# A graph network's node update: TensorE turns the new rows one step later, ahead of the second products

## The reference

```
agg = segment_sum(messages, dst)
u   = mish(concat([h, agg]) @ W3 + b3)        # h: 10000 x 512
y   = h + (u @ W4 + b4)
x   = x + layernorm(y) * gamma + beta
h   = relu(layernorm(x))                      # input of the fourth layer, L3
out = x + relu(batchnorm(mean_agg(h) @ W_l.T + b_l + h @ W_r.T))
```

## Time and profile before

| what | value |
|---|---|
| median of 3 runs | 2826.0 us (2825.43 to 2830.35) |
| the profiled execution's own time | 2847.13 us |
| its span | 2845.4 us, granted TensorE clock 0.943 |
| busy: TensorE, VectorE, ScalarE, GpSimd | 2446.0, 1907.5, 1520.3, 1122.4 us |
| node update, steps of pairs 4 to 28 | 13.03 us for a pair |
| node update, steps in the zone | 14.45 us for a pair |

### The profile page before, as it was taken

How to read it: one execution, slowest core, us unless ns; L and a number is a source line. 1 busy time by engine, 2 the same in 40 slices (tenths; PEclk the granted TensorE clock), 3 DMA queues, 4 the chain that set the end, 5 groups by cost and what they waited for, 6 DMA issues and landing times. The chain is left out here.

```text
span 2845.4 us, 45119 instructions
## 1 busy us (share of the span) xinstructions
PE 2446.0 (86%) x13421; PEld 1424.2 (50%) x13421; DVE 1907.5 (67%) x4612; ACT 1520.3 (53%) x2246; POOL 1122.4 (39%) x1908
## 2 busy tenths in 40 slices
PE   1648898799789999898978979989999997998954
PEld 1435564344344455444544537766666664444443
DVE  8838886687568866898863436668888887223343
ACT  7637774354335533454335756668888775232280
POOL 1567744254333322555545511124444444001155
PEclk9669999999999999999988989999999998999976
DMA  5545543488559888666544332233333444001187
GB/s 200 204 139 158 156 143 122 124 202 179 117 131 222 203 150 173 222 220 217 185 157 125 103 95 76 90 105 120 121 118 121 142 142 154 3 6 52 45 289 292
DMA packets 374158, 413.92 MB, mean 145 GB/s; under 512 B 192822, under 2 KB 232037, under 8 KB 371182
## 3 DMA queue, kind: packets, MB, share of 16 engines
q1 hardware_dynamic: 347918, 337.27, 40.2%
q0 software_dynamic: 26080, 74.68, 9.0%
HBM read 172.47 MB, written 198.18 MB: 130 GB/s over the span
## 5 line engine op out<-in xcount | busy, mean ns | idle before, releaser
L215 PE MATMUL s_ps_z<-own_weights,slots 128*128 128x512 f16 x2844 | 638.9, 382 | 7.8 <-PEq L163 7.8
L215 PEld LDWEIGHTS s_ps_z<-own_weights,slots 128*128 128x128 f16 (+1 forms) x2844 | 279.1, 98 | 325.0 <-issue 18.0
L1756 ACT ACTIVATE s_g<-s_g,s_rn 128x512 f32<-128x512 f32 x237 | 169.8, 716 | 226.9 <-POOL s_rn L1615 226.7
L1615 POOL TENSOR_TENSOR s_rn<-s_em,minus_half 128x1 f32<-128x1 f32 x237 | 179.7, 758 | 219.0 <-DVE s_em L1684 211.6
L1665 DVE SCALAR_TENSOR_TENSOR s_g<-s_ps_z,s_f,s_bias 128x512 f32<-128x512 f32 x237 | 177.9, 751 | 103.4 <-PE s_ps_z L215 90.8
L2565 PE MATMUL u_ps_z<-slots,weights 128*128 (+2 forms) x1920 | 215.9, 273 | 4.2 <-PEq L163 4.2
L2701 PE MATMUL z_ps_z<-slots,weights 128*128 128x512 f16 (+1 forms) x960 | 212.3, 381 | 2.4 <-PEq L163 2.4
L2565 PEld LDWEIGHTS u_ps_z<-slots,weights 128*128 128x128 f16 x1920 | 186.4, 98 | 26.9 <-issue 4.4
L2670 DVE BATCH_NORM_STATS2 z_stats<-slots 128x6 f32<-128x512 f32 (+1 forms) x76 | 52.2, 687 | 187.9 <-ACT slots L2687 187.9
L1675 DVE SCALAR_TENSOR_TENSOR s_junk<-s_g 128x512 f32<-128x512 f32 x237 | 164.5, 694 | 4.1
L215 PE MATMUL s_ps_z<-s_wn,s_aT 128*128 128x512 f16 x720 | 165.2, 379 | 1.8 <-DVE s_aT L1498 1.8
(11 more groups left out here) (435 smaller groups left out, 5558.2 us busy)
## 6 DMA issues: line engine op xcount, KB each, us to landing
h_rows<-s_g SPq DMA_DIRECT2D x237, 256.0 KB, 2.7
x_rows<-q_x SPq DMA_DIRECT2D x79, 256.0 KB
s_halves<-x_rows SPq DMA_DIRECT2D x79, 256.0 KB
x_rows<-s_halves SPq DMA_DIRECT2D x79, 256.0 KB
u_x<-x_rows SPq DMA_DIRECT2D x79, 256.0 KB
x_rows<-u_x SPq DMA_DIRECT2D x79, 256.0 KB
h_rows<-u_h SPq DMA_DIRECT2D x79, 256.0 KB
weights<-x_rows SPq DMA_DIRECT2D x79, 256.0 KB
```

The source lines that it names most:

```text
L215: ins = nc.tensor.matmul(out_ap, a(c), w[:, part * size + c * n:part * size + (c + 1) * n], start=first and c == 0 and m == 0, stop=stop a ...
L1615: nc.gpsimd.tensor_tensor(out=self.rn[b][:, :], in0=self.em[b][:, :], in1=minus_half[:, :], op=POW).then_inc(self.s_rn, 1)
L1756: nc.scalar.activation(self.g[b][:, :], self.g[b][:, :], ACT.Relu, scale=self.rn[v.buf(2)][:, 0:1]).then_inc(self.s_h, 1)
```

## The change

Three engines' step lists change; nothing else does. TensorE turns pair s - 3 instead of s - 2 in step s, and does so right behind `update`, ahead of the two `second`. ScalarE makes the high halves of pair s - 3, and ahead of `hi_u` instead of behind it. VectorE makes the low halves of pair s - 3 at the same place in its list. `next_rows`, SyncE and GpSimd stay as they are, and so do all waits and buffers. `by_pairs` already runs to step 42, in which pair 39 is now turned.

```diff
@@ VectorE
                     of_pair(v, -1, add_messages(0))
                     of_pair(v, -1, add_messages(1))
-                    of_pair(v, 2, lo)
+                    of_pair(v, 3, lo)
                     of_pair(v, 1, residual, (1,))
@@ ScalarE
                     whole_pair(v, 0, log)
                     whole_pair(v, 0, tanh)
                     of_pair(v, 2, next_rows, (1,))
+                    of_pair(v, 3, hi)
                     whole_pair(v, 0, hi_u)
-                    of_pair(v, 2, hi)
@@ TensorE
                 def step(v):
                     whole_pair(v, 0, update)
+                    of_pair(v, 3, turn)
                     of_pair(v, 1, second)
-                    of_pair(v, 2, turn)
```

## The result

| what | before | changed |
|---|---|---|
| median, same chip, 4 runs each | 2825.72 us (2824.8 to 2830.35) | 2933.18 us (2929.66 to 2936.91) |
| ratio | | 1.037, 95% interval 1.0355 to 1.0385 |
| the profiled execution's own time | 2847.13 us | 2936.16 us |
| its span and granted clock | 2845.4 us, 0.943 | 2934.4 us, 0.927 |

The changed kernel is slower by 107.5 us. On another chip, with the kernel before beside it, it took 2921.54 us against 2825.84: 1.0338 (1.032 to 1.0356), so 96 us. The forecast was 92 us more, with a range of 64 to 124.

The account below looks back on a forecast made before the run. Before, TensorE's own 13.03 us of work set the step; after, a 15.10 us ring would. 2826.0 + 80 (74.7 for the steps, 5.2 at the end) + 12 for the clock = 2918 us, range 2890 to 2950.

Parts of the forecast that it names:

- Both waits: TensorE idle before L226 until VectorE's L2475; ScalarE idle 3 to 4 us before the first L893 until the turn.
- The ring, 15.10: Outside the zone: turn, next_rows, mish, hi, hi_u, lo_u, residual, centred, lo, next turn set the step at 15.10 us.
- The zone, 16.65: In the zone four message operations ahead of lo add 1.55 us to the 15.10, making the step 16.65 us.
- The clock, 12 us: TensorE's clock falls behind pauses in the zone, not outside; 0 to 21 us over 10 zone steps, 12 taken.
- the 0.9 of the prediction: Slack of 0.9 us in a step: second ends at 8.2 us behind the release, hi_u is due at 9.14.
- 1.84 us without a fall: An earlier TensorE pause of 1.84 us left the clock at 1.00; used against falls outside the zone.
- The drain, 5.2: At the stage's end the last second waits for turns needing both lo: 4.2 us later, 5.2 with hi.
- Rival 2: Ring open, lo never late for the turn, only hi ahead of hi_u costs: 10 plus 12 us, 2848; chance 0.10.
- Rivals 4 and 5: 4: faster, the turn's zone wait on ScalarE goes, 2807 to 2815, chance 0.04; 5: nothing changes, 2826, chance 0.03.
- Rival 3: Clock falls outside the zone too, every second step: 10 to 25 us, 2928 to 2952, middle 2935; chance 0.15.
- the dear 2927: Total time with the ring as forecast and the dearest clock falls in the zone; 2906 with no fall.
- The one through GpSimd: Ring from residual through GpSimd (3.03 us) to next_rows and back, 13.5 us; judged not to decide.

Follow-up runs that it names:

- the filler: Changed kernel plus 5 extra 512-column products a step (11 in the zone) on TensorE between update and the turns; 2907.72 us, 1.0292 to the kernel before.
- single part undone: Changed kernel with one edit taken back: both next_rows behind tanh, 2898.47 us, 1.0235; or hi behind hi_u again, 2900.56 us, 1.0239.
- the lag alone: Kernel before with turn, hi and lo three pairs behind instead of two, each at its old place; 3089.16 us, 1.0923.

## Why the prediction was right, point by point

- **The bound before, and the waits.** TensorE's own 13.03 us set the step, and the pause of 1.20 before the turn was no loss: the experiment that gained in the zone moved VectorE's messages and left that turn alone. Both waits that the prediction named are in the trace, and TensorE's 90% too. Of its signs one did not come: the pause in the zone is 2.23 us, not over 3, since the slow products fill the rest; at full clock, with the filler, it is 2.54 of filler and 0.78 of idle time.
- **The ring, 15.10.** Measured 15.20 and 15.39 by turns with the clock at full; of the 0.19 of every second step 0.12 lies between `hi_u` and `lo` and 0.06 between the turn and `next_rows` (kernel with filler in the pause, steps of 2058.04 and 2073.26), and why it comes by turns stays open. In the kernel with filler in the pause the 25 steps took 382.39 us (2279.19 - 1896.80), forecast 377.5. That `next_rows`, `hi` and `lo` are on the ring is shown by the runs that move them; for the others it rests on the rows, which follow each other without a gap.
- **The zone, 16.65.** At full clock 16.53. The 11 steps from 28 to 38, two of them with half the messages, took 180.56 us with the filler, forecast 181.7. The messages ahead of `lo` cost 1.32 (2378.30 to 2379.62), not 1.55.
- **The clock, 12 us.** The total was near, the place was not. Against the kernel with filler in the pause the changed one took 389.13 - 382.39 = 6.7 us more outside the zone, 188.44 - 180.56 = 7.9 in it and 3.8 in the drain, 18.4; on the other chip 6.3 + 5.5 + 3.8 = 15.6, and 13.8 by the medians. I had put all 12 into the zone and nothing outside or into the drain, so that they add up to about as much is in part luck. The clock falls outside too, in about every second or third step: 9 of 24 steps took over 15.7 us. The price per fall was nearly right: 16.0 against 15.3 is 0.7 a step, just under the 0.8 to 2.1. In the zone both `second` took 8.42 us (2364.39 to 2372.81) instead of 6.83, 1.59 of work late; less the 0.9 of the prediction that leaves 0.7, and `hi_u` came 0.66 late. The argument "1.84 us without a fall" rested on a single pause, and a pause of this length goes both ways. Two steps of the changed kernel that follow each other, each with its turn and 6 us behind it:

```profile
2122.26 1.32 PE L226 MATMUL u_ps_t<-ident,u_h 128*128 128x128 f32 x8 [1.90 <-DVE slots L2475]
2123.00:2129.00 6.00, 6.00 (x40) 3.11 (x41) 2.97 (x8) 5.85 (x8) 1.72 (x6) 1.00 0.24 87
...
2137.53 1.25 PE L226 MATMUL u_ps_t<-ident,u_h 128*128 128x128 f32 x8 [1.80 <-DVE slots L2475]
2138.50:2144.50 6.00, 6.00 (x31) 2.80 (x30) 1.65 (x5) 5.94 (x8) 1.07 (x4) 0.72 0.24 87
```

Behind the longer pause the clock stays at 1.00, behind the shorter one it is 0.72. What parts the two, no run here shows.
- **The drain, 5.2.** Measured 8.7, of which 3.8 goes away with the filler, though that drops its own products into the drain's steps as well; 4.9 is left, near the forecast. The turns before the last pairs took 1.94 us for 8 transposes instead of 1.2, behind a pause of 5.47:

```profile
2497.97 1.94 PE L226 MATMUL u_ps_t<-ident,u_h 128*128 128x128 f32 x8 [5.47 <-DVE slots L2475]
```

- **The sum.** 78.5 for the ring up to step 39 (562.95 - 484.46, with the filler; forecast 74.7), 14.6 for the clock up to there, 8.7 for the drain: 101.8. The stages behind the node update took 16 of the 21 us by which the profiled execution of before stood above its median (by comparison with the changed kernel's), so to carry the difference over unscaled was right. The 15.5 us by which 107.5 exceeds the forecast are 3.8 of ring, 2.6 of clock, 3.5 of drain and 5.6 from outside what the sum covers.
- **The rivals.** Rival 2 fell, since `lo` was late in every step. Rivals 4 and 5 fell. Rival 3's mechanism came in beside the ring, with some 6.5 us where 17 stood. That 2933.18 lies next to its 2935 is chance: the clock as a whole cost only 2.6 us more than the 12 up to step 39. (The upper end of that rival, 2952, adds its 25 us to the dear 2927 and not to 2918.)
- **What the prediction missed** without harm to its number: the ring just under the first, 14.4 through `u_hi`. The one through GpSimd it had, at 13.5; with `lo` ahead of the `residual` it is 14.7. These two are why no single part undone gives much more than a third back. By the wait of `next_rows`, which reaches back as many tiles as `u_h` has buffers, more of them should open the first ring without any reordering; that was not tried.

The Trainium skill ("TensorE: Matmul & The Clock Gate", Part 4, PE-mode transpose) says that transposes do not count as busy for the clock as products do. The runs agree in so far as a pause of 1.80 to 1.90 us with the turn behind it was often followed by a low clock, if not always, and one of 0.8 with the same turn was not. They do not part the turn's share from the pause's: with the lag alone a pause of 4.82 us with no turn between it and `second` was followed by a low clock as well, 0.55 over the next 6 us.

The Trainium skill ("Perfetto Trace Analysis", Optimization Strategy) says that the same gap over and over on the engine that should be full can mean too few buffers for the next tile. The repeated gap before L226 (25 times in 25 steps) fits that: two buffers each of `u_ps_t` and `u_h`, and the wait is for a buffer to be freed. No run here has more buffers.

## What to carry to other kernels

A stage that is moved a step back gains slack only if the buffers that it holds last as long; with two buffers and engines that work in order, follow each wait once around the step and add up the ring, with what stands ahead of it on every engine. Then do the same for the next rings, without the first: only what lies under all of them is won. A sum of distances between rows of the old kernel gave such a ring to within 1.5% (377.5 us forecast for 25 steps, 382.39 at full clock).

## What the runs showed of the hardware

- Whether the granted clock falls behind a pause of TensorE and a group of transposes is not a matter of the pause's length alone: in two steps of the changed kernel that follow each other, 1.90 us without a fall (1.00) and 1.80 with one (0.72).
- Useless products can pay: five to eleven 512-column products (1.24 to 2.54 us) in the pause made the kernel 13.8 us faster. Another 1.35 us of products a step, placed at the update, kept the clock at 1.00 outside the zone; in the zone, where they left 1.61 to 1.85 us of pause, it was 0.96.
- What slow products cost depends on the slack beside them: in the changed kernel's zone both `second` took 1.59 us more (8.42 against 6.83) and the step became 0.7 longer; in the kernel with the lag alone they took 2.6 more (9.40), and as they lie on its ring without slack, all of it stands in the step.
